# Conv 2 of a three-convolution graph network: the residual made one pair ahead, and SyncE's order of loads changed

## The reference, cut to what matters

```python
h = relu(layernorm(x))                       # N = 30000 rows of D = 512
x = x + block(h)                             # two convolutions, below
h = relu(layernorm(x));  x = x + gcn_conv(h, W3, b3)

def gcn_conv(h, W, b):                       # 30000 edges, and a self-loop on each node
    msg = (dinv[s] * dinv[d])[:, None] * (h @ W)[s]
    return segment_sum(msg, d) + b

def block(h):
    residual = h
    h = gelu(layer_norm(gcn_conv(h, W1, b1), gamma1, beta1))
    h = layer_norm(gcn_conv(h, W2, b2), gamma2, beta2)
    return gelu(h + residual)
```

## Time and profile before

| | before |
|---|---|
| time, median of 3 runs (lowest, highest) | 3271.37 us (3271.06, 3271.75) |
| the profiled execution | 3272.66 us |
| its span | 3270.8 us |
| busy in the span: PE, DVE, ACT, POOL | 2904.5, 2548.5, 2053.4, 2062.6 us |
| TensorE's granted clock, mean | 0.99 |
| conv 2, first to last gelu | 1345.71 to 2375.23 us |

### The profile page before, as it was taken

How to read it: one execution, slowest core, us unless ns; L and a number is a source line. 1 busy time by engine, 2 the same in 40 slices (tenths; PEclk the granted TensorE clock), 3 DMA queues, 4 the chain that set the end, 5 groups by cost and what they waited for, 6 DMA issues and landing times. The chain is left out here.

```text
span 3270.8 us, 60605 instructions
## 1 busy us (share of the span) xinstructions
PE 2904.5 (89%) x16427; PEld 2433.2 (74%) x16427; DVE 2548.5 (78%) x6373; ACT 2053.4 (63%) x3083; POOL 2062.6 (63%) x1615
## 2 busy tenths in 40 slices
PE   8233369999999999799999999999969999999999
PEld 2122258888888888688888888888758888888888
DVE  9899968888888888699999999999934454444544
ACT  0266556777767776689888989999933333333333
POOL 0122257777777775688888888888755555555553
PEclk9999999999999999899999999999979999999999
DMA  3399987888888786799999999999789999999996
GB/s 133 149 382 418 411 237 217 214 216 217 214 219 215 213 215 168 241 317 326 320 315 314 324 318 316 316 322 319 263 240 287 286 290 289 286 289 286 288 287 209
DMA packets 304977, 890.18 MB, mean 272 GB/s; under 512 B 67209, under 2 KB 67707, under 8 KB 304922
## 3 DMA queue, kind: packets, MB, share of 16 engines
q1 hardware_dynamic: 189082, 681.53, 60.0%
q0 software_dynamic: 115840, 208.01, 26.8%
HBM read 652.74 MB, written 307.71 MB: 294 GB/s over the span
## 5 line engine op out<-in xcount | busy, mean ns | idle before, releaser
L840 POOL DMA_INDIRECT gathered<-H,idx x826 | 1155.5, 1399 | 514.9 <-issue 237.7
L1228 PE MATMUL out<-Whi,ahi 128*128 128x512 f32 x2832 | 778.9, 397 | 39.8 <-ACT out L923 38.5
L914 ACT ACTIVATE ahi<-agg 128x1024 fp32r<-128x1024 f32 x354 | 360.8, 1019 | 642.6 <-PE agg L1219 642.6
L1228 PE MATMUL out<-Wlo,ahi 128*128 128x512 f32 x2832 | 761.6, 391 | 0.0
L1228 PE MATMUL out<-Whi,alo 128*128 128x512 f32 x2832 | 739.4, 390 | 0.1
L1228 PEld LDWEIGHTS out<-Wlo,ahi 128*128 128x128 f32 x2832 | 533.4, 188 | 116.0
L1228 PEld LDWEIGHTS out<-Whi,ahi 128*128 128x128 f32 x2832 | 509.9, 189 | 146.0 <-ACT out L923 50.9
L1228 PEld LDWEIGHTS out<-Whi,alo 128*128 128x128 f32 x2832 | 531.5, 188 | 110.9 <-DVE alo L1039 0.5
L1031 DVE TENSOR_TENSOR vlo<-gathered,vhi 128x512 fp32r<-128x512 f32 x354 | 243.0, 686 | 319.4 <-ACT vhi L908 319.4
L1039 DVE TENSOR_TENSOR alo<-agg,ahi 128x1024 fp32r<-128x1024 f32 x354 | 429.5, 1213 | 57.6 <-ACT ahi L914 56.9
L923 ACT ACTIVATE out<-vec,sqrt_deg 128x512 f32<-128x512 f32 x708 | 458.0, 681 | 16.4 <-PEq L750 9.8
(11 more groups left out here) (162 smaller groups left out, 3730.1 us busy)
## 6 DMA issues: line engine op xcount, KB each, us to landing
gathered<-H SPq DMA_DIRECT2D x351, 512.0 KB, 6.1
H<-ho SPq DMA_DIRECT2D x250, 512.0 KB, 4.3
x<-in_x_dram SPq DMA_DIRECT2D x165, 512.0 KB, 8.1
X<-x SPq DMA_DIRECT2D x117, 512.0 KB
x<-X SPq DMA_DIRECT2D x117, 512.0 KB, 7.4
out_dram<-conv SPq DMA_DIRECT2D x117, 512.0 KB
H<-x SPq DMA_DIRECT2D x48, 512.0 KB, 9.8
gathered<-H,idx POOLq DMA_INDIRECT x826, 5.4
```

What stands on the lines that cost most here:

```text
L840: pool.indirect_dma_start(rows, None, H[q][0:end, :], bass.IndirectOffsetOnAxis(ap=idx[p.slot(4)][:, c:c + 1], axis=0), bounds_check=end - ...
L914: nc.scalar.activation(Ahi[p.slot(2)][:, :], Agg[p.slot(2)][:, :], ACT.Copy)\
L1228: m = nc.tensor.matmul(Out[2 * p.slot(2) + j][:, :], a[p.slot(2)][:, c:c + P], w[q][:, f, :], start=False, stop=stop and f == KD - 1, skip ...
```

## The change

In conv 2 alone:

- ScalarE makes R one pair ahead of its turn (pair n+1 in turn n), where it was two (pair n+2 in turn n). Ahead of turn 0 it makes R of pair 0 only.
- SyncE issues the load of x first in a turn (pair n+2, as before), then the store of x2, then the load of the own rows of pair n+5, then the store of h.

```diff
@@ -813,7 +813,7 @@
                             for k in range(fetched, 4):
                                 load_self(0, p.after(k), k)
                             load_self(0, p.after(4), 4)
-                        if has(known, 5):
+                        if not second and has(known, 5):
                             load_self(known, p.after(5), 5)
                         if has(known, 2):
                             load_x(known, p.after(2), 2)
@@ -823,6 +823,8 @@
                             fetch_x()
                         if has(known, -1):
                             store_x(known, p.after(-1), -1)
+                        if second and has(known, 5):
+                            load_self(known, p.after(5), 5)
                         if has(known, -lag):
                             store_h(known, p.after(-lag), -lag)
                     turn(sp, body)
@@ -985,8 +987,7 @@
                             if second:
                                 high(p.after(1))
                                 over_high(p.after(2))
-                                for k in range(2):
-                                    relu_x(k, p.after(k))
+                                relu_x(0, p)
                                 over_high(p.after(3))
                                 seed(1, p.after(1))
                         if second:
@@ -1000,8 +1001,8 @@
                                 seed(of(known, 2), p.after(2))
                             if has(known, -2):
                                 relu_x2(of(known, -2), p.after(-2))
-                            if has(known, 2):
-                                relu_x(of(known, 2), p.after(2))
+                            if has(known, 1):
+                                relu_x(of(known, 1), p.after(1))
                             if has(known, 4):
                                 over_high(p.after(4))
                             return
```

## The result

| | before | after |
|---|---|---|
| time, median of 4 runs | 3271.22 us | 3623.61 us |
| the profiled execution's span | 3270.8 us | 3622.3 us |
| conv 2, first to last gelu | 1029.5 us | 1382.4 us |
| one turn in conv 2, mean from gelu 2 to gelu 115 | 8.82 us | 11.87 us |

What follows compares the result with a forecast made beforehand. It took hand-overs between four nearly full engines to bound conv 2, and a new loop of 11.21 us per turn against 8.80 to add 273.8 us to 3271.4, giving 3545 us, range 3495 to 3595.

Steps and rivals of the forecast that it cites:

- What bounds the kernel: Conv 2: TensorE leads, four engines nearly full, so hand-overs matter; turn 8.80 us, TensorE busy 8.45 us of it.
- the lead lost: ScalarE to GpSimd in conv 2: the residual's 6.7 us lead goes, as it is made one 8.8 us turn later.
- the forecast 2.8: TensorE in conv 2: would stand still some 2.8 us in every turn.
- The loop: Conv 2: residual, adds, power, `normal`, gelu, next residual close a loop over one turn, 11.21 us against 8.80.
- the third term: GpSimd in conv 2: adds start to power end, 4.77 us, of it 2.54 adds, 1.03 overflow gather, 1.04 power.
- the sum: Conv 2: 111 gelus at 11.21 us, slightly shorter last turns; gelu 117 comes 273.8 us later, 3545 us in all.
- The bounds of the prediction: Conv 2 loop: 10.75 us a turn with signals at nothing, 11.7 us with waits costing 0.24 us each.
- The rival of a longer loop: Conv 2: waits over 0.2 us each, or late gather data; 11.7 to 12.3 us a turn, 3600 to 3670; chance 0.05.
- SyncE's edits at 0 us: SyncE in conv 2: earlier x load and later own-rows load change nothing; x worth at most 38.5 us through TensorE.
- rival of the gain: Conv 2: x wait goes, TensorE sets the turn at 8.45 us; 40 us less, 3231 us; chance 0.04.
- TensorE's clock: Conv 2, rival: stops lower the clock; nothing changes unless whole turns run at 1.2 GHz, then 4200 us; chance 0.02.

Runs made afterwards that it cites:

- e2: Kernel before, with only ScalarE's residual moved to one pair ahead and SyncE's order as before: 3622.4 us, ratio 1.1071.
- e3: Changed kernel, with GpSimd's power of pair n ahead of the overflow gather of pair n+4 instead of behind it: 3500.75 us, ratio 1.0701.
- e7: Changed kernel, with ScalarE's residual of pair n+1 right behind the gelu of pair n, ahead of seed and `relu_x2`: 3354.26 us, ratio 1.025.
- e8: Changed kernel, with VectorE's `x2_sum` taking its first operand from a PSUM tile instead of x in SBUF: 3539.14 us, ratio 1.083.
- e6: Changed kernel, with GpSimd's power of pair n ahead of the adds of pair n: 3456.75 us, ratio 1.0563.
- e9: Changed kernel, with GpSimd's power ahead of the adds and `x2_sum`'s first operand from PSUM: 3339.83 us, ratio 1.022.
- e1: Kernel before, with only SyncE's new order; ScalarE makes the residual two pairs ahead as before: 3241.67 us, ratio 0.9907.
- e5: Changed kernel, with VectorE's `x2_sum` replaced by a copy of y reading one SBUF operand, without addition and row sum: 3558.03 us, ratio 1.0873.

## Why the prediction was wrong

**What bounds the kernel; the lead lost:** right. Who waits for whom came out as forecast, except one: TensorE waits for `sv` (302.4 us), not for the seed. VectorE makes `sv` only after `normal`, and TensorE needs it earlier in its turn than the seed. That the amount, 2.7 us a turn, is near the forecast 2.8 is luck: the turn is 0.66 us longer than forecast, and TensorE's work in it takes 9.16 us at the lower clock instead of 8.45.

**The loop:** right in its members (e2, e3, e7), wrong in one term. By the steps of the prediction, forecast against the row: gelu to residual 3.63, 3.60; residual to the adds' start 0.88, 0.90; adds to power end 4.77, 5.50; signal to VectorE 0.16, 0.25; `x2_scale` to the end of `normal` 1.69, 1.70; last signal 0.08, 0.03. The sum is 11.98 for 11.21, and 0.73 of the 0.77 is the third term: 0.44 in the adds, 0.27 in the gather. Over the run: gelu 2 came 1.0 us late (conv 2 itself began 0.9 us later), the 113 turns up to gelu 115 took 11.87 each, 1341.5 us for the 1264.3 of the sum (111 x 11.21 and 2 x 10.0), the last two 0.8 more. Together 79 us, the whole miss. With the collision taken out (e8) adds start to power end is 4.79 us (2005.88 to 2010.67), where the sum had 4.77, and its 3545 stands against 3539.

**The failed step, then,** is the term of 4.77 us read from the earlier trace rows: the mechanism was right, and the adds and the gather in it were mis-sized, at 5.50 us measured. It was read in a turn in which the adds ran, apart from two small instructions, beside VectorE's `low` and `stats`, which take an operand from PSUM (`agg`, `out`):

```profile
1946.69 1.20 DVE L1039 TENSOR_TENSOR alo<-agg,ahi 128x1024 fp32r<-128x1024 f32 x1
...
1947.82 1.28 DVE L1047 BATCH_NORM_STATS2 small<-out 128x6 f32<-128x512 f32 x2
```

There the adds started 1.15 us after the end of `normal`; now they start 4.5 us after it (gelu starts with that end, at 2009.60, the adds at 2014.10), next to `x2_sum`, which reads two operands from SBUF. The bounds of the prediction moved the signals and left these durations fixed, so the range ended at 3595. Even that end was too high for its own reason: it adds 0.24 us twice to a sum that already holds 0.08 and 0.16 for these signals. With 0.24 in their place the loop is 11.45 us, and the end is near 3573. The rival of a longer loop had the size (11.7 to 12.3 us a turn, 3600 to 3670 us) but two other reasons: signals of over 0.2 us each, which took 0.10, 0.25 and 0.03, and late data of the gathers, which nobody waited for.

The trace of before could have told. Two of VectorE's groups there, both of two elements a partition:

```profile
L1112 DVE SCALAR_TENSOR_TENSOR small<-small,eps_c 128x2 f32<-128x2 f32 x102 | 32.7, 320 | 0.0
...
L1105 DVE SCALAR_TENSOR_TENSOR small<-small,ones 128x2 f32<-128x2 f32 x102 | 16.4, 161 | 3.5
```

The first takes twice as long; it is the one that falls beside the adds: in the turn of the earlier trace rows it starts at 1904.23 and ends at 1904.55, and the adds end at 1904.52. The Trainium skill says it outright (SBUF — State Buffer, Who interferes with whom): a VectorE instruction with two SBUF inputs contends with a GpSimd instruction that reads SBUF, and whoever comes first keeps the other out for the whole instruction. The traces agree: in e6, e7, e8 and e9 the small instruction ends within 0.03 us of the add that it stands beside (adds and instruction: 2011.34 and 2011.35, 2008.01 and 2008.03, 2008.42 and 2008.44, 2012.77 and 2012.80).

**SyncE's edits at 0 us:** right within this change (e2 against after: 3622.4 and 3623.61). Right also that the own rows can be asked for later: no wait for them stands in the tables of after and e1. By itself that half is worth 30 us (e1), inside the 38.5 us named as its most. In the *rival of the gain* the time of 3231 us assumed this and no cost from ScalarE; the kernel that has it is e1, at 3241.67.

**TensorE's clock:** it did fall, to 0.93 over the stretch, with stops of 2.7 us a turn on average and 4.2 at most, and it made no difference: 1009.49 us of work in 1308 leaves room, and e8, with the same 0.97 over the execution as after, comes within 6 us of the sum.

## What to carry to other kernels

A stage that hands its result over one turn later turns a hidden dependence into a loop over one turn: add up that loop in the order of each engine's list, with everything that stands between its members, and compare it with the turn. When a step slides against another engine, don't take its duration along: look at what it will run beside, and at where the operands of both lie. Of two edits made together, ask for each alone; here one by itself was worth 30 us and the other cost 351.

## What the runs showed of the hardware

A GpSimd add on SBUF and a VectorE instruction with two operands in SBUF don't overlap: each waits for the other's current instruction to end (`x2_sum` 1.76 for 0.68 us, the adds 2.98 to 3.55 for 2.54, a two-element instruction 1.11 for 0.16). With one operand in PSUM they run side by side, `x2_sum` at 0.68 us and the adds at 2.54 (e8). Lying in SBUF isn't enough: in e7 `mean_var`, which has one SBUF operand, runs within the adds (2005.50 to 2008.01) at its usual length, two in 0.24 us:

```profile
2006.70 0.24 DVE L1057 BATCH_NORM_AGGREGATE small<-small 128x2 f32<-128x6 f32 x2
```

The copy of e5, also with one operand, did lengthen the adds, to 2.73 us; which mode it ran in no run shows. A loop can close through such a collision, with no wait in the table that names it (e6). GpSimd's issue of an indirect gather takes 1.30 us where it starts beside the end of `x2_sum` (after) and 1.03 where nothing (e8) or `centre`, with one operand in PSUM, stands beside it (e7); no run holds `x2_sum` in place beside the gather and moves its operand, so the cause of this part is not isolated.
